# Grouped attention: a step's first piece of values is multiplied between its scores and its first two turns of probabilities

## The reference, cut to what matters

```
q = rms_norm((layernorm(x) @ Wq) per head)
k = rms_norm((ctx @ Wk) per head);  v = ctx @ Wv
probs = softmax(q @ k.T * scale)     # 256 x 1601 for each head
x = x + (probs @ v) @ Wo
```

## Time and profile before

| what | value |
|---|---|
| median of 3 runs | 1695.53 us (1695.09 to 1697.14) |
| the profiled execution's own time | 1699.32 us |
| its span in the trace | 1697.5 us |
| TensorE busy | 1455.1 us, 86% of the span |
| VectorE busy | 1160.9 us, 68% |
| ScalarE busy | 984.3 us, 58% |
| GpSimd busy | 568.0 us, 33% |
| first scores of the grouped attention start at | 508.41 us |
| last scores start at | 1593.48 us |

### The profile page before, as it was taken

One profiled execution on the slowest core, in us unless ns is written; L12 is line 12 of the kernel. 1 busy time (PEld: TensorE's weight loads), 2 busy tenths in 40 slices (PEclk: granted clock), 3 DMA queues, 4 the chain that ended last, 5 costly groups with the idle time before them and its releaser, 6 DMA issues. The chain is left out here.

```text
span 1697.5 us, 27527 instructions
## 1 busy us (share of the span) xinstructions
PE 1455.1 (86%) x10079; PEld 1363.0 (80%) x10082; DVE 1160.9 (68%) x2329; ACT 984.3 (58%) x2062; POOL 568.0 (33%) x470
## 2 busy tenths in 40 slices
PE   5778547888858989899999989999989999999945
PEld 4677546877747989899999989999989999999823
DVE  4553466888856777667676766777766677777657
ACT  3445216787735656566666566665656656666535
POOL 2223313453244522343223343233324333322134
PEclk8988857999979999999999999999999999999968
DMA  5132118889812302011011110110201101000010
GB/s 190 64 115 102 35 60 278 293 292 321 269 56 53 80 4 68 20 39 41 7 41 44 31 50 9 40 41 8 68 20 38 42 8 41 20 8 23 26 50 25
DMA packets 83547, 128.05 MB, mean 75 GB/s; under 512 B 17108, under 2 KB 63352, under 8 KB 83032
## 3 DMA queue, kind: packets, MB, share of 16 engines
q1 hardware_dynamic: 78856, 113.84, 20.8%
q0 software_dynamic: 4560, 12.46, 2.8%
HBM read 114.28 MB, written 11.99 MB: 74 GB/s over the span
## 5 line engine op out<-in xcount | busy, mean ns | idle before, releaser
L1843 ACT ACTIVATE ga_pT<-ga_ps_t 128x512 fp32r<-128x512 f32 (+1 forms) x512 | 243.7, 516 | 255.0 <-PE ga_ps_t L2077 254.7
L1978 DVE TENSOR_TENSOR ga_pT<-ga_ps_t,ga_pT 128x512 fp32r<-128x512 f32 (+1 forms) x512 | 280.2, 583 | 95.7 <-ACT ga_pT L1843 93.6
L1851 ACT ACTIVATE ga_probs<-ga_ps_s,ga_neg_max 128x1200 f32<-128x1200 f32 (+1 forms) x256 | 235.5, 927 | 91.8 <-DVE ga_neg_max L1999 91.4
L2077 PE MATMUL ga_ps_t<-all_eye,ga_probs 128*128 128x128 f32 (+1 forms) x1664 | 227.0, 274 | 9.7 <-DVE ga_pT L1978 9.6
L2077 PEld LDWEIGHTS ga_ps_t<-all_eye,ga_probs 128*128 128x128 f32 (+1 forms) x1664 | 193.0, 141 | 19.6 <-DVE ga_pT L1978 12.4
L1994 DVE TENSOR_REDUCE ga_part_max<-ga_ps_s 128x1 f32<-128x1200 f32 x128 | 178.8, 1397 | 12.4 <-PE ga_ps_s L2028 11.1
L1745 POOL TENSOR_TENSOR ga_oT<-ga_out_n,ga_oT 128x256 fp32r<-128x256 f32 x64 | 47.5, 742 | 394.8 <-ACT ga_oT L1866 394.8
L2028 PE MATMUL ga_ps_m<-ga_pT,ga_v 128*128 128x256 f32 (+1 forms) x1248 | 174.1, 287 | 3.3 <-DVE ga_pT L1978 3.2
L2028 PE MATMUL ga_ps_m<-ga_pT,side_v 128*128 128x256 f32 (+1 forms) x1248 | 174.8, 287 | 0.5 <-DVE ga_pT L1978 0.3
L2028 PE MATMUL ga_ps_t<-side_w_kv,side_encT 128*128 128x256 f32 (+1 forms) x1170 | 162.2, 288 | 13.7 <-DVE ga_pT L1978 8.4
L2028 PEld LDWEIGHTS ga_ps_t<-side_w_kv,side_encT 128*128 128x128 f32 (+1 forms) x1170 | 144.8, 186 | 23.2 <-DVE ga_pT L1978 11.2
(11 more groups left out here) (293 smaller groups left out, 2649.3 us busy)
## 6 DMA issues: line engine op xcount, KB each, us to landing
ex_raw<-in_L_ffn_packed SPq DMA_DIRECT2D x63, 704.0 KB, 5.8
side_w_q_raw<-in_L_xattn_Wq SPq DMA_DIRECT2D x16, 512.0 KB, 4.9
side_w_q_raw<-in_L_xattn_Wo SPq DMA_DIRECT2D x16, 512.0 KB, 4.6
ga_inv_rows<-ga_inv_row SPq DMA_DIRECT2D x64, 128.0 KB, 3.0
mix_y_rows<-ex_y SPq DMA_DIRECT2D x63, 128.0 KB, 4.1
side_enc<-in_ctx_turned SPq DMA_DIRECT2D x12, 512.0 KB, 5.6
ca_keys<-in_ctx_turned SPq DMA_DIRECT2D x12, 464.0 KB, 6.7
ca_cache<-in_ctx SPq DMA_DIRECT2D x4, 1024.0 KB, 5.5
```

Source lines behind the costliest of these rows:

```text
L1843: nc.scalar.activation(dst(HI), src, ACT.Copy, scale=scale).then_inc(read, 1)
L1851: nc.scalar.activation(dst, src, ACT.Exp, bias=neg_max[:, n % 2:n % 2 + 1], accum_out=half_sum[:, n % 4, k:k + 1]).then_inc(exped, 1)
L1978: nc.vector.tensor_tensor(dst(LO), src, f32(dst(HI)), ALU.subtract).then_inc(empty, 1)
L2077: mm = nc.tensor.transpose(out[0:top, i * P:(i + 1) * P], probs[step % PB][:, tile * P:tile * P + top], eye[:, :])
```

## The change

In `step_plan`, `values[0:1]` moves from behind `turns[0:2] + early` to directly behind the scores. Nothing is added or taken away, and `values[1:2]`, `late` and `turns[2:4]` keep their order.

```
@@ -1474,7 +1474,7 @@
         early, late = prepared(n) if n < N + DRAIN - 1 else ([], [])
         if n == N + DRAIN - 1:
             late = [("y", t, GROUPS - 1) for t in range(QT)]
-        return (([("scores", 0, n)] if n < N else []) + turns[0:2] + early + values[0:1] + late[:1] + values[1:2]
+        return (([("scores", 0, n)] if n < N else []) + values[0:1] + turns[0:2] + early + late[:1] + values[1:2]
                 + turns[2:4] + late[1:])
```

## The result

The changed kernel took 1742.4 us (median of 4 runs, 1738.14 to 1747.87) against 1695.31 (median of 4) for the kernel before: ratio 1.0277, 95% interval 1.0247 to 1.0308. The forecast was 1743.5. Its profiled execution took 1738.14 us, with a span of 1736.3 against 1697.5.

The account below looks back on a forecast made before the run. The prediction took TensorE to bound the stage, with short stalls at the end of a relay through ScalarE and VectorE. Full groups 42 us, last group and drain 4, group 0 2: 48 on 1695.5 gave 1743.5 us, range 1718 to 1768.

Parts of the forecast that it names:

- The frame: The stage is bound by TensorE; a reordering can win only its 2 us idle a group, or lengthen its stalls.
- (a): After T (scores' end) ScalarE's exponential starts late, costing 0.74 us in s2, 0.35 s3, 0.57 s6, 1.08 s7.
- By step: A full group loses 3.23 us over its steps, 2.15 in the three groups ahead of a new row.
- (b): In s1 the turns no longer cover the values' wait for VectorE's last turn: +0.49 us a group.
- (c): Groups with little in them: last group and drain lose 4 us (1 for the drain), group 0 loses 2.
- The sum: 42 us in full groups plus 4 and 2 in light ones make 48, added to the 1695.5 median.
- The signs: Trace shows waits of 1.2 us at s2's second kv, 1.6 at s7's last kT, 0.9 in s1; groups 72.
- Absorbed lateness: ScalarE has idle time and catches up, so only the lost s1 cover and drain count: 1703 us; chance 0.10.
- The clock: TensorE's clock falls after s7's longer stall, 2 us in 11 groups, 22 on top: 1766 us; chance 0.06.
- No effect: Gains and losses over the kernel cancel: 1695.5 us; chance 0.03.
- Faster: Values fill TensorE's waits for banks ahead of turns, 7.1 us in four places: 1688 us; chance 0.04.

Follow-up runs that it names:

- e6: Kernel before, TensorE's order kept, with a ScalarE copy of 896 or 1344 columns ahead of each exponential to delay it: 1723.82 us against 1698.59, ratio 1.0157.
- e5: Kernel before with the first piece of values directly behind the scores in s1 only: 1707.23 us against 1698.59, ratio 1.0059.
- e4: Kernel before with the first piece of values directly behind the scores in s7 only: 1707.22 us against 1697.64, ratio 1.0051.
- e3: Kernel before with the first piece of values directly behind the scores only in s0, s4 and s5: 1700.54 us against 1697.64, ratio 1.0016.
- e7: Kernel before with both pieces of values behind the q entry in s1: 1697.01 us against 1698.59, ratio 1.0002.

## Why the prediction was right, point by point

- **The frame** (TensorE bounds the stage, and the loss is in its short stalls): right. Its work is unchanged, and 1.88 of the 2.22 us that group 8 is longer are idle time (the whole program's modelled busy time rose from 1455.1 to 1460.2). The one part of the program that the change touches holds all of the loss.
- **(a), the exponential late by the length of the values' piece**: right in kind, and e6 shows it as a cause, since the delay alone, with TensorE's order untouched, brings s2, s6 and s7 back to within 1.7 us of their losses. By the prediction it starts at T + 2.8 and 2.85, measured T + 2.67 and 2.70. What was mis-sized is the length of the piece right behind scores, 1.07 instead of 1.14 us for nine matmuls and 1.42 instead of 1.52 for twelve; and ScalarE's exponential starts 0.12 and 0.11 ahead of the recorded end of its copies, where I had taken off 0.07.
- **By step**, over groups 1 to 14, forecast and measured: s2 14 x 0.74 = 10.4 and 9.3; s7 11 x 1.08 = 11.9 and 10.3; s6 14 x 0.57 = 8.0 and 5.7; s3 14 x 0.35 = 4.9 and 1.4; s0, s4 and s5 nothing and 0.3. s6 is smaller by the earlier exponential (0.1 each) and since group 1's s6 is held by VectorE's work for the experts anyway. In s3 most of the lateness is absorbed and the stall changed its place: the first qT waits 0.47 and the second 0.27, where the second alone had waited 0.86. These are the two, and VectorE's turn between them:

```profile
1112.02 0.66 PE L2065 MATMUL ga_ps_t<-all_eye,ga_qn 128*128 128x128 f32 x4 [0.47 <-DVE ga_v L1966]
1112.21 0.87 DVE L1978 TENSOR_TENSOR ga_pT<-ga_ps_t,ga_pT 128x512 fp32r<-128x512 f32 x2
1112.94 0.66 PE L2065 MATMUL ga_ps_t<-all_eye,ga_qn 128*128 128x128 f32 x4 [0.27 <-DVE ga_pT L1978]
```

  T is 1106.01 here, so VectorE's turn is at T + 6.20, with no idle time left in front of it. It was at T + 6.09 behind 0.63 of idle time. The exponential came 0.84 later (T + 2.71 and 1.87), not 0.98, and of that 0.11 was left where 0.35 was forecast.
- **(b), the lost cover in s1**: 14 x 0.49 = 6.9, measured 4.5. Alone (e5) it is 4.9 in s1. The step that failed is that I read one group and gave its wait to all fourteen: groups 1, 3, 7 and 11 had none. I also left out that s7's delay lets the output weights arrive earlier, seen from s0, and takes 4.5 us out of s1 (e4), and that s0's own late turns put a wait into every group. The wait in s1 of group 8 was to be the whole 0.95 and is 0.54 (2.82 from start to start, less 2.28), and the four groups without a wait pay most (groups 3, 7 and 11 have an s1 of 8.2 us instead of 7.5).
- **(c), the light groups and the drain**: forecast 6, measured 2.9 + 2.9 + 3.8 = 9.6. The last group was forecast at 3 and group 0 at 2. The drain was mis-sized, 1 against 3.8, and the 1 had no row under it. This is its first wait in the changed kernel, and the busy time by engine from 1644 to 1648, columns as in the earlier trace rows:

```profile
1637.56 2.00 PE L2028 MATMUL ga_ps_m<-ga_pT,ga_v 128*128 128x256 f32 x9 [1.99 <-DVE ga_pT L1978]
```

```profile
1644.00:1648.00 4.00, 3.31 (x15) 3.32 (x16) 0.63 (x1) 0.00 (x0) 0.29 (x1) 0.59 0.23 37
```

  From the last scores to the output projection it takes 27.9 us instead of 22.6 (to 1656.68 from 1628.81, and to 1616.10 from 1593.48). In this stretch the waits for VectorE's turns add up to 5.2 us in three places; before, they were 1.9 and 1.4. The first line is the changed kernel's, the others are the kernel before's:

```profile
PE ga_ps_m L2028 <- DVE ga_pT L1978: 5.2, 3, 2.0
```

```profile
PE ga_ps_m L2028 <- DVE ga_pT L1978: 1.9, 2, 1.5
PE ga_ps_t L2077 <- DVE ga_pT L1978: 1.4, 2, 0.9
```

  With the values in front, three steps of the drain begin with a wait for the last turn of the step before, here 1.99 us: no late entries and no scores stand between, so the prediction's "elsewhere the last turn is out before the scores end" doesn't hold here. The granted clock was 0.50, the lower level, from 1637.9 to 1641.3, behind this wait, and eight transposes took 1.56 us (1639.36 to 1640.92) instead of 0.79; from 1644 to 1648 its mean was 0.59. Before, it was 1.00 up to the output projection. So 1.9 us of the 5.3 are longer waits, and the lower clock in the same stretch can hold most of the rest; no run takes the two apart. The output projection's 24 matmuls then took 3.1 us instead of 4.6, since it was there that the clock had been low before, and 3.8 are left.
- **The sum**: 48 forecast; 41.1 in the steps of the two profiled executions, 38.8 in their spans, 47.1 in the medians. The forecast was made for the trace, and there it was 7 too high: 42.0 against 31.5 in the full groups, 6 against 9.6 in the rest. The profiled execution of the kernel before was longer than its four runs (1699.3) and that of the changed kernel the shortest (1738.1), which makes the 8 between spans and medians. That 1743.5 meets the median within 1.1 us is therefore luck; that it is 2 to 3% slower, and by which steps, is not. What the other 6 us of the medians are made of isn't shown.
- **The signs**: every wait grew where it was said, and each less than said. The rows of PE show 0.89 ahead of s2's second kv, 1.21 ahead of s7's last kT and 0.37 ahead of the values in s1, for 1.2, 1.6 and 0.9 forecast; group 8 took 70.97 for 72.
- **The rivals.** Absorbed lateness: no, though true in s0, s4 and s5 (e3) and for most of it in s3. The clock: not in group 8, 1.00 in both. It fell in the drain, and where a long stall had been before: in s6 of group 1 and at the start of each new row. There it can stay low longer, a mean of 0.66 from 1001 to 1011 us in the changed kernel and 0.83 from 990 to 1000 before, both at the start of group 7. That costs far less than the 22 us of this rival: s0, the step behind such a stall, is 0.5 us longer in all. (Its price a group was about right: twelve score matmuls at the lower level took 4.15 us, 1273.25 to 1277.40 before, 1.9 more than 2.28, where I had 1.7.) The sentence of the Trainium skill ("TensorE: Matmul & The Clock Gate", "A second HAM failure mode: psum-queue depth-cycling") isn't borne out by group 8, whose six stalls of 0.27 to 1.23 us left the clock at 1.00. No effect: no, the ratio's interval starts at 1.0247. Faster: no, the waits ahead of turns stayed as they were, 7.1 us in four places, as this line of the changed kernel's waits of TensorE (600 to 1600 us) shows:

```profile
PE ga_ps_t L2077 <- DVE ga_pT L1978: 7.1, 4, 2.3
```

## What to carry to other kernels

In a ring that several engines empty in program order, an entry's place decides not only when its producer runs, but when everything behind its copy does: here an exponential that stood behind two copies, and everything behind the exponential. Before moving work on the busiest engine, look for what the next engine queues behind the thing you delay, and follow it to the next bank that the busy engine waits for. Read more than one group before you multiply: s1's wait differed from group to group, and four of fourteen had none. And look at where the stalls are first: the same reading that priced this change pointed at s2's kv and s3's qT, and moving those two gained 1.1%.

## What the runs showed that I had not expected

Values right behind scores took 1.07 us for nine matmuls, start to start, and behind transposes 1.14; twelve took 1.42 (1073.95 less 1072.53), 1.52 where they began behind a wait (1090.13 less 1088.61), and 1.50 behind transposes without one (1021.64 less 1020.14, s3 of group 7 before). What makes the difference I haven't tried. And taking one stall away can gain nothing where the next entry of the ring waits for the same instruction: e7 took the wait away ahead of the values, and it came back at q in the next row of the trace, ended by the same instruction of VectorE.
